# Routing weights through memory instead of through a product: one change to a GRU scan with a mixture of experts beside it

## The reference

```python
def cell(h, x):
    gi = x @ W_ih + b_ih
    gh = h @ W_hh + b_hh
    ...
    h_new = (1.0 - z) * n + z * h
    return (h_new, h_new)
...
scores = jax.nn.sigmoid(jnp.dot(xf, gate_w.T))
topv, topi = jax.lax.top_k(scores, 2)
topv = topv / topv.sum(axis=-1, keepdims=True)
dw = jnp.zeros((T, E)).at[jnp.arange(T)[:, None], topi].add(topv)
y0 = _mlp(xf, sw1, sw2, sw3)
def step(y, ws):
    e1, e2, e3, we = ws
    return (y + _mlp(xf, e1, e2, e3) * we[:, None], None)
```

## Time and profile before

| | us |
|---|---|
| median of 3 runs (lowest, highest) | 2738.11 (2737.35, 2738.44) |
| the profiled execution's own time | 2739.84 |
| its span in the profile | 2737.9 |
| first to last scan product (L1152) | 652.0 to 2584.5 |
| PE busy | 2545.8 (93%) |
| DVE, ACT, POOL busy | 1973.0, 1051.1, 1164.3 |
| moved by DMA | 209.39 MB |

### The profile page before, as it was taken

How to read it: one execution, slowest core, us unless ns; L and a number is a source line. 1 busy time by engine, 2 the same in 40 slices (tenths; PEclk the granted TensorE clock), 3 DMA queues, 4 the chain that set the end, 5 groups by cost and what they waited for, 6 DMA issues and landing times.

```text
span 2737.9 us, 159456 instructions
## 1 busy us (share of the span) xinstructions
PE 2545.8 (93%) x69506; PEld 1992.5 (73%) x69506; DVE 1973.0 (72%) x7088; ACT 1051.1 (38%) x3585; POOL 1164.3 (43%) x2972
## 2 busy tenths in 40 slices
PE   5777778787999999999999999999999999999999
PEld 2333333445888788888888888888888888888888
DVE  3767777774666777777787778878777777877722
ACT  4271625263333333333333333333333333333333
POOL 1232221222332455455545555554555555455454
PEclk9799989899999999999999999999999999999999
DMA  4100000001111233233333333333332333222344
GB/s 168 36 22 17 2 17 3 2 3 33 39 50 48 79 96 95 83 106 93 96 96 95 94 87 106 93 96 99 93 98 83 106 93 97 89 90 85 85 153 133
DMA packets 144746, 209.39 MB, mean 76 GB/s; under 512 B 16432, under 2 KB 86320, under 8 KB 143664
## 3 DMA queue, kind: packets, MB, share of 16 engines
q1 hardware_dynamic: 142896, 195.01, 23.3%
q10 hardware_dynamic: 1152, 4.19, 0.4%
HBM read 185.51 MB, written 13.63 MB: 73 GB/s over the span
## 4 chain that ended last, share of the span: by engine, by line
PE 70%; DVE 3%; issue 1%; POOL 1%; ACT 1%; DVEq 0%; POOLq 0%; ACTq 0%
PE ps L1152 27%; PE ps L1187 24%; PE ps L1202 12%; PE ps L1164 6%; PE ps L1176 2%; POOL hidf L844 0%; DVE turn_n L1033 0%; DVE turn L1036 0%; DVE fresh L1046 0%; DVE hcur L1048 0%; DVE hcur L1051 0%; DVE npre L1039 0%; ACT cand L940 0%; DVE h L1049 0%; DVE up L1020 0%
## 5 line engine op out<-in xcount | busy, mean ns | idle before, releaser
L1152 PE MATMUL ps<-whh,hcur 128*32 128x128 f16 x49152 | 791.5, 220 | 23.8 <-DVE hcur L1051 12.3
L1152 PEld LDWEIGHTS ps<-whh,hcur 128*32 128x32 f16 x49152 | 694.3, 97 | 147.0 <-DVE hcur L1051 119.4
L1187 PE MATMUL ps<-hb,w 128*128 128x256 f16 x6400 | 781.8, 273 | 0.0
L1187 PEld LDWEIGHTS ps<-hb,w 128*128 128x128 bf16 x6400 | 602.9, 98 | 95.1 <-DMA w<-in_w 0.3
L836 POOL COPY hb<-hcur 128x32 f16<-128x32 f16 x512 | 169.8, 332 | 664.2 <-DVE hcur L1051 664.2
L1202 PE MATMUL ps<-hid,w 128*128 128x256 f16 x3200 | 428.3, 273 | 2.2 <-POOL hid L856 1.8
L933 ACT ACTIVATE r<-ur 128x16 f32<-128x16 f32 x512 | 110.6, 216 | 825.5 <-DVE ur L1027 825.5
L1202 PEld LDWEIGHTS ps<-hid,w 128*128 128x128 bf16 x3200 | 312.3, 98 | 39.8 <-issue 3.0
L844 POOL TENSOR_TENSOR hidf<-up 128x256 f32<-128x256 f32 x400 | 291.8, 730 | 98.1 <-POOL hid L856 50.5
L856 POOL TENSOR_TENSOR hid<-hidf,hid 128x256 f16<-128x256 f32 x400 | 269.0, 673 | 62.3 <-ACT hid L929 62.3
L1024 DVE STREAM_TRANSPOSE turn<-ps 128x128 f32<-128x128 f32 x512 | 161.8, 316 | 179.4 <-PE ps L1152 168.9
(11 more groups left out here) (143 smaller groups left out, 3277.7 us busy)
## 6 DMA issues: line engine op xcount, KB each, us to landing
w<-in_w SPq DMA_DIRECT2D x400, 256.0 KB, 2.7
w<-in_w SPq DMA_DIRECT2D x400, 128.0 KB, 2.7
gi_scratch<-gis SPq DMA_DIRECT2D x72, 128.0 KB, 1.7
spare<-gi_scratch SPq DMA_DIRECT2D x36, 128.0 KB, 2.8
gi<-gi_scratch SPq DMA_DIRECT2D x36, 128.0 KB, 2.7
x2T<-in_xT SPq DMA_DIRECT2D x4, 1024.0 KB, 7.7
out<-xo ACTq DMA_DIRECT2D x8, 512.0 KB, 4.4
stage<-in_W_hh SPq DMA_DIRECT2D x1, 3072.0 KB, 11.1
```

What stands on the lines that cost most here:

```text
L1152: mm = pe.matmul(ps[j * COLS:(j + 1) * COLS, bank, 0:P], hcur[:, k], whh[:, s, k, at:at + P], start=(k + s == 0), stop=(k == KT - 1 and s ...
L1187: mm = pe.matmul(ps[:, UB[u], w * TOK:(w + 1) * TOK], w13[:, u, w, k], hb[:, f % 2, s, k].rearrange("p b t -> p (b t)"), start=(w + k + s ...
```

## The change

The weights stay float32: `dwT` is 16x256, copied once from PSUM (`weights_out`, ACT, step 7), and ACT itself sends it to a scratch tensor in memory, `dw_scratch`. SP then loads for each expert chunk the row of its expert into all 128 partitions of one of six slots of `wsb` (128 KB written); where a chunk holds the end of one expert and the start of the next (12 of 44), two loads do it. The load for chunk c + 1 stands in SP's queue behind `w2_load` of chunk c. `weigh`, `share`, `weights_low`, the table `owner`, its load at the start and the zeroing of `dwT` go, and `DOWNS` no longer counts the pairs.

```diff
-HIDS, W2S = 10, 12
+HIDS, W2S, WSS = 10, 12, 6
...
+        dw_dram = nc.dram_tensor("dw_scratch", (2, E, TOK), F32, kind="Internal").ap()
...
-        owner = sb("owner", [P, NCH - SCH, P], BF16)
-        dwT = sb("dwT", [P, TOK], F16)
-        wsb = sb("wsb", [P, 2, 2 * TOK], F32)
+        dwT = sb("dwT", [E, TOK], F32)
+        wsb = sb("wsb", [P, WSS, TOK], F32)
...
-            shares = sum(1 for at in WEIGH if EXPERTS <= at <= i)
-            total = UP * NCH - UPS[EXPERTS - 1] + DOWN * NCH - LATE + NWG - 1
-            downs = -(-total * (i - EXPERTS + 1) // (TB - EXPERTS)) - (UPS[i] - UPS[EXPERTS - 1]) - shares
+            total = UP * NCH - UPS[EXPERTS - 1] + DOWN * NCH - LATE
+            downs = -(-total * (i - EXPERTS + 1) // (TB - EXPERTS)) - (UPS[i] - UPS[EXPERTS - 1])
...
+        NX = NCH - SCH
+        SPLIT = [min(P, (x * P // TOPI + 1) * TOPI - x * P) for x in range(NX)]
...
-            for dst, src in ((gwf[:], a["gate"]), (ne[:], a["ne"]), (identf[:], a["identf"]), (owner[:], a["owner"])):
+            for dst, src in ((gwf[:], a["gate"]), (ne[:], a["ne"]), (identf[:], a["identf"])):
...
+            def wsb_load(f, x):
+                xn = f * NX + x
+                if xn >= WSS:
+                    before = xn - WSS
+                    sp.wait_ge(up2_done, before // NX * NCH + SCH + before % NX + 1)
+                sp.wait_ge(dwT_sent, (f + 1) * 16)
+                e, s = x * P // TOPI, SPLIT[x]
+                sp.dma_start(wsb[0:s, xn % WSS], dw_dram[f % 2, e:e + 1].to_broadcast([s, TOK])).then_inc(wsb_in[xn % WSS], 16)
+                if s < P:
+                    sp.dma_start(wsb[s:P, xn % WSS], dw_dram[f % 2, e + 1:e + 2].to_broadcast([P - s, TOK])).then_inc(wsb_in[xn % WSS], 16)
...
                     w2_load(n)
+                    if SCH <= c + 1 < NCH:
+                        wsb_load(f, c + 1 - SCH)
                     if c % 4 == 2 and f + 2 < NBLK:
...
-            nc.gpsimd.memset(dwT[:], 0.0).then_inc(dwT_zero, 1)
...
-            def share(f, p):
-                n = f * NWG + p
-                act.wait_ge(weighed, n + 1)
-                act.wait_ge(up2_done, f * NCH + SCH + 2 * (p - 1))
-                nc.scalar.copy(wsb[:, (p + SCH // 2) % 2], ps[:, WB, :]).then_inc(wsb_done, 1)
...
-            def weights_high(f):
+            def weights_out(f):
                 act.wait_ge(turned, f + 1)
-                nc.scalar.copy(dwT[0:E], ps[0:E, WB, 128:128 + TOK]).then_inc(dwT_hi, 1)
+                need(act, dwT_sent, f * 16)
+                nc.scalar.copy(dwT[:], ps[0:E, WB, 128:128 + TOK]).then_inc(dwT_out, 1)
+                act.wait_ge(dwT_out, f + 1)
+                act.dma_start(dw_dram[f % 2], dwT[:]).then_inc(dwT_sent, 16)
...
                 if c >= SCH:
-                    dve.wait_ge(wsb_done, f * NWG + (c - SCH) // 2 + 1)
-                    nc.vector.tensor_tensor(up2[:], ps[:, UB[c % 2], TOK:2 * TOK], wsb[:, (c // 2) % 2, (c % 2) * TOK:(c % 2 + 1) * TOK],
-                                            ALU.mult).then_inc(up2_done, 1)
+                    xn = f * NX + c - SCH
+                    dve.wait_ge(wsb_in[xn % WSS], loads_until(xn) * 16)
+                    nc.vector.tensor_tensor(up2[:], ps[:, UB[c % 2], TOK:2 * TOK], wsb[:, xn % WSS], ALU.mult).then_inc(up2_done, 1)
...
-            def weights_low(f):
-                dve.wait_ge(dwT_hi, f + 1)
-                nc.vector.tensor_tensor(dwT[LOW:LOW + E], ps[0:E, WB, 128:128 + TOK], dwT[0:E], ALU.subtract).then_inc(dwT_lo, 1)
...
-            def weigh(f, p):
-                if p == 0:
-                    pe.wait_ge(dwT_hi, f + 1)
-                    pe.wait_ge(dwT_lo, f + 1)
-                need(pe, wsb_done, f * NWG + p)
-                for c in range(2):
-                    mm = pe.matmul(ps[:, WB, c * TOK:(c + 1) * TOK], owner[:, 2 * p + c], dwT[:],
-                                   start=(c == 0), stop=True, skip_group_check=True)
-                mm.then_inc(weighed, 1)
```

More of the change, by code:

```diff
@@ L18 @@
 NCH = SCH + E * TOPI // P
-NWG = (NCH - SCH) // 2
 PAIRS = TB // 2
-LOW = 64
 HALF = 2.0 ** 15
@@ L50, in build @@
         gi_dram = nc.dram_tensor("gi_scratch", (NBLK, P, M3, B * TB), F32, kind="Internal").ap()
+        dw_dram = nc.dram_tensor("dw_scratch", (2, E, TOK), F32, kind="Internal").ap()
         nc.disable_value_cache = True
         attention(nc, a, ps, x2T, whh, wih, bias, spare, h)
-        scan_and_ffn(nc, a, ps, x2T, whh, wih, bias, spare, h, gi_dram)
+        scan_and_ffn(nc, a, ps, x2T, whh, wih, bias, spare, h, gi_dram, dw_dram)
 def attention(nc, a, ps, x2T, whh, wih, bias, spare, h):
@@ L651, in _, with scan_and_ffn @@
                 pass
-def scan_and_ffn(nc, a, ps, x2T, whh, wih, bias, spare, h, gi_dram):
+def scan_and_ffn(nc, a, ps, x2T, whh, wih, bias, spare, h, gi_dram, dw_dram):
     with ExitStack() as ctx:
@@ L703, in scan_and_ffn @@
         route = sb("route", [P, 2, E], F32)
-        init_in, gw_hi, gw_ready, dwT_zero, h_zero = sem("init_in"), sem("gw_hi"), sem("gw_ready"), sem("dwT_zero"), sem("h_zero")
+        init_in, gw_hi, gw_ready, h_zero = sem("init_in"), sem("gw_hi"), sem("gw_ready"), sem("h_zero")
         gi_in = [sem("gi_in0"), sem("gi_in1")]
@@ L715, in scan_and_ffn @@
         r_ready, z_ready, cand_ready, copied = sem("r_ready"), sem("z_ready"), sem("cand_ready"), sem("copied")
-        up_done, weighed, down_done = sem("up_done"), sem("weighed"), sem("down_done")
-        wsb_done = sem("wsb_done")
+        up_done, down_done = sem("up_done"), sem("down_done")
+        wsb_in = [sem("wsb_in%d" % n) for n in range(WSS)]
         sg_done, up1_done, up2_done, hidf_done, hid_hi, hid_lo = (
@@ L720, in scan_and_ffn @@
         logit_done, logit_ready, scored, rstep = sem("logit_done"), sem("logit_ready"), sem("scored"), sem("rstep")
-        routed, turned, dwT_hi, dwT_lo = sem("routed"), sem("turned"), sem("dwT_hi"), sem("dwT_lo")
+        routed, turned, dwT_out, dwT_sent = sem("routed"), sem("turned"), sem("dwT_out"), sem("dwT_sent")
         passed = sem("passed2")
@@ L749, in scan_and_ffn @@
         GATE = [2, 3, 4, 6, 7, 8] + [EXPERTS + n * (TB - EXPERTS) // (NCH - SCH) for n in range(NCH - SCH)]
-        WEIGH = [GATE[SCH + 2 * p] - 1 for p in range(NWG)]
         gate_at = [[c for c in range(NCH) if GATE[c] == i] for i in range(TB)]
-        weigh_at = [[p for p in range(NWG) if WEIGH[p] == i] for i in range(TB)]
         LEFT = [4, 3, 4, 4, 3, 5, 4, 3, 2]
@@ L772, in scan_and_ffn, with loads_until @@
         assert DOWNS[-1] == DOWN * NCH - LATE
+        NX = NCH - SCH
+        SPLIT = [min(P, (x * P // TOPI + 1) * TOPI - x * P) for x in range(NX)]
+        def loads_until(xn):
+            return sum(1 if SPLIT[v % NX] == P else 2 for v in range(xn % WSS, xn + 1, WSS))
         block = ctx.enter_context(nc.Block())
@@ L968, in _ @@
                         if i == TURN:
-                            weights_high(f)
+                            weights_out(f)
                         if i == RESULT + 1 and f >= 1:
@@ L976, in _ @@
                             sigmoid(f, c)
-                        for p in weigh_at[i]:
-                            share(f, p)
                     if g + 1 < S:
@@ L983, in _ @@
             for c in range(NCH):
-                if c >= SCH and c % 2 == 0:
-                    share(f, (c - SCH) // 2)
                 sigmoid(f, c)
@@ L1004, in split_router @@
             def split_router():
-                dve.wait_ge(init_in, 4 * 16)
+                dve.wait_ge(init_in, 3 * 16)
                 nc.vector.tensor_copy(gw[:, :, 0], gwf[:]).then_inc(gw_hi, 1)
@@ L1122, in _ @@
                             next(routing)
-                        if i == TURN + 1:
-                            weights_low(f)
                         if i == RESULT and f >= 1:
@@ L1223, in logits @@
                 if f == 0:
-                    pe.wait_ge(init_in, 4 * 16)
+                    pe.wait_ge(init_in, 3 * 16)
                     pe.wait_ge(gw_ready, 1)
-                    pe.wait_ge(dwT_zero, 1)
                     pe.wait_ge(g_out, GATES)
-                need(pe, wsb_done, f * NWG)
+                need(pe, dwT_out, f)
                 for t in range(2):
@@ L1257, in _ @@
                         turn_weights(f)
-                    for p in weigh_at[i]:
-                        weigh(f, p)
                     take(ups, UPS[i] - (UPS[i - 1] if i else 0))
@@ L1272, in _ @@
             for c in range(2, NCH):
-                if c >= SCH and c % 2 == 0:
-                    weigh(f, (c - SCH) // 2)
                 take(ups, UP)
@@ L1312 @@
     r = np.arange(P)
-    owner = np.zeros((P, E * TOPI), w13.dtype)
-    for e in range(E):
-        owner[e, e * TOPI:(e + 1) * TOPI] = 1
-    owner[LOW:LOW + E] = owner[0:E]
     sel = np.repeat((r[:, None] % 32 == 4 * np.arange(QT) + r[:, None] // 32)[:, :, None], P, axis=2).astype(np.float16)
@@ L1331 @@
         "gate": rows(np.asarray(L0_ffn_gate_w).T[unit]),
```

(2 more changed lines are left out.)

1 line of the change is left out of this document (removed).

## The result

The changed kernel takes 2782.07 us (median of 4 runs, 2776.72 to 2789.74) against 2737.73 for the kernel before beside it: 44 us more, ratio 1.0164, 95% interval 1.014 to 1.0188. The forecast was 2727, its range ended at 2752. The profiled execution is the longest of the four, 2789.74 with a span of 2787.7, so the trace shows some 8 us more loss than the median. Two later executions that took 6656 and 6249 us (one of four in experiment 4, one of ten in experiment 8), where the others of the same kernel took under 2800, are left out of the medians.

A forecast was written before the change was run, and what follows sets the result against it. TensorE was taken to bound the kernel, scan steps lying within 0.2 us of both PE's work and the recurrence. Terms -21.1 - 4.8 + 1.5 + 12 + 1 = -11.4 on 2739.8 gave 2728.4, at the median 2727; range 2711 to 2752.

The forecast's parts named there:

- Contention: +1 us: Mid-scan: PE's 22.7 us of unexplained waits may grow with a fifth more DMA traffic; +1 us.
- The broadcast loads, +12: Scan: rows land in 3.3 us, a third of 105 narrow chunks stall DVE by 0.35 us each; +12 us.
- The products in the scan, -21.1: Scan: without the owner pairs, 21 steps a block shorten and more nine-unit steps follow each other; -21.1 us.
- step 7, +1.5: ACT's wait and DMA issue in step 7 cost 2.8 us, removing weights_low in step 8 gives 1.3; +1.5 us.
- The two floors: Scan step: PE's work, 3.75 us with ten units, and the recurrence, about 3.57 us whatever PE does.
- the count of turned steps: Scan, steps 10 to 63: 21 steps a block turn from 3.75 into 3.63 us, leaving 22 of ten units.
- Pass 7, -4.8: Last pass, no recurrence: 22 owner pairs removed at 0.22 us each; -4.8 us.
- Pass 7, late rows: 0: Last pass: rows come a microsecond late each time, but downs and ups run later, so it costs 0.
- the 2.4 that the forecast gave as cover: Last pass: up products wait for L1020 of two chunks before, with 2.4 us; longer delays stall each chunk.
- PE waits for w13 or POOL's low half in pass 7: Last pass: a sign that, if it appeared, would make the prediction wrong.
- Slower: Rival: surcharge by rows or queued reads of one address; 2750 us at 3.7 us landing, 2778 at 4.3; chance 0.20.
- All hidden: Rival: broadcasts land like any load, in 2.7 to 3.0 us, giving 2715 us; chance 0.24.

The follow-up runs named there:

- experiment 4: Kernel before, plus the same number of broadcast loads at the same places, into a tile nobody reads: 2793.12 us, 54.2 above before.
- experiment 8: Changed kernel with w2 loaded only twelve times and then reused, all broadcast loads kept: 2734.06 us, 4.6 below before.
- experiment 1: Changed kernel with only the first six broadcast loads, later chunks reusing those rows: 2719.94 us, 19.0 below before.
- experiment 2: Changed kernel with each load reading 128 different rows of 1 KB instead of one row 128 times: 2741.62 us, 2.7 above before.
- experiment 6: Changed kernel, loads issued one chunk earlier and, in the scan, only after SP waits for the next step's z products: 2767.19 us, 29.1 above before.
- experiment 7: Changed kernel with each load reading 512 B from each of 128 different rows: 2728.27 us, 9.8 below before.
- experiment 5: Changed kernel with each broadcast load issued one chunk earlier: 2780.89 us, 42.8 above before.
- experiment 9: Kernel before with one owner product per expert, 8 pairs a pass instead of 22, no memory round trip: 2727.74 us, 10.4 below before.
- experiment 3: Changed kernel with broadcast rows of 512 B instead of 1 KB, still from one address: 2769.49 us, 30.6 above before.

## Why the prediction was wrong

**The step that failed is "Contention: +1 us".** It named the right row, PE's waits "that nothing in the profile explains, mid-scan", and priced the growth at 1 us for a fifth more traffic. Against experiment 1 the loads cost 63 us: 21.7 for bytes (experiment 2) and 41.6 for the one address. In the window the issue waits grew by 53 us, in the scan's products, where each one holds the recurrence. The trace puts a price on them: measured against the medians of experiment 1 at the same positions, the 142 steps of after with such a stall are 69.0 us longer and all other steps together 9.8; in experiment 1 itself it is 13.6 us in 41 steps, and 4.7. The error was to scale an unexplained wait by mean traffic. Half of the row's 22.7 us lies in block 0 besides, in waits of at most 0.5 us, where no expert's weights are loaded. The growth goes with what the DMA engines have to do at the moment when TensorE's next instructions are due, as the next paragraph shows.

What is shown of that, and what is inferred. Shown: loads that touch nothing of TensorE's make its scan stall (experiment 4), less queued at once makes fewer stalls (6, 7, 8), late rows make at most a small part of the loss (4, 5), and every stall stands where a new block of 256 instructions begins. From the trace, read packet by packet, between block 1 and the end of the scan: nearly nine stalls in ten (36 of 42 before, 126 of 142 after) end 1.25 to 1.6 us after a 16 KB packet of the instruction queue ends, and such a packet takes 1.08 us on the mean before and 1.07 after. So the packets aren't slower, they begin late. From the moment when TensorE enters one block to the begin of the packet for the next, the median is 1.17 us where no stall follows and 1.90 where one does. And it depends on the data: after, where the DMA engines were busy with data for under a tenth of the first microsecond of that time, a stall followed in 7 of 89 cases, and where it was four tenths or more, in 135 of 270. With different rows (experiment 2) it was 62 of 272 in the busier case, and 28 of 222 before, so how busy the engines are isn't all of it. Inferred: that the late packets stood behind data in their own DMA engine. The trace doesn't say what a packet waited for.

The Trainium skill (Runtime: NRT & Kernel Launch, Instruction fetch mechanics) has the sequencer refill its instruction memory by a DMA queue of its own in 16 KiB blocks of 256 instructions, the cost of a crossing "mostly hidden". The trace agrees on the block: q8 has 392 packets and 6.42 MB in the window, 16.4 KB each, and 6.42 MB over the 99,715 products and weight loads are 64 bytes each, so the queue is TensorE's. The stalls at every 256th instruction say the same. On the cost it agrees only while the data queues are short: 11.4 us at 94 GB/s, 64.3 with the change.

**The broadcast loads, +12, on DVE.** The landing was right: 3.3 forecast, 3.4 in the scan.

```profile
L805 SPq DMA_DIRECT2D wsb<-dw_scratch x298: 324/376/2198, 935.2 to 2576.6; - x149
...
DMA to landing us min/median/max: 1.8/3.4/4.9
```

The prediction's estimate by the row-pitch figures of the Trainium skill (DMA: Bandwidth & Descriptors, Latency and other measured facts) was 3.1; the trace is slower than that. Experiment 2 shows that the surcharge of 0.7 us over different rows is real. The waits that followed were right in sum too, 11.1 us, though in 21 longer waits and not 35 of 0.35. What they cost was less. Experiment 5 removes them and gains 1.5 us by the medians, some 10 at the most. In the trace, 17 of the 21 fall in steps without a stall of TensorE; they are 7.7 us of waits, and these 17 steps are 3.9 us longer than the medians of experiment 1. So the item of +12 was about right as a sum of waits and too large as a price, and it wasn't where the loss lay. What stands ahead of a load matters here too: without w2 (experiment 8) the row lands in 3.3 us instead of 3.5, and DVE's waits fall to 1.5 us.

**The products in the scan, -21.1, and step 7, +1.5.** By the steps' medians, seven times their sum fell from 1669.3 us to 1649.8 in experiment 1: -19.5 where -19.6 was forecast. The two floors hold, and so does the count of turned steps: by the medians of experiment 1, 22 of the 54 late positions take 3.7 us or more, 44 before. The item for step 7 came near by luck: of its +2.8 for ACT's write 1.3 came (step 8 went from 3.62 to 3.80 us, seven times 0.18), and its -1.3 for `weights_low` didn't come at all (the step behind it stayed at 3.58). Some of the gain was lost again to irregular steps, 18.3 us in experiment 1 against 12.4, which the forecast had put at nothing.

**Pass 7, -4.8.** From the last scan start to the end it is 150.0 us in experiment 1, 154.7 before: -4.7, right.

**Pass 7, late rows: 0.** Here it is 159.7 in the changed kernel and 155.1 in experiment 5, where nearly all rows come in time. DVE waited 83.7 us in 38 waits between 2590 and 2790, nearly all of it covered as argued, because the downs run behind. The cover ran out at some split chunks. Timeline of after:

```profile
2660.97 0.38 SPq L805 DMA_DIRECT2D wsb<-dw_scratch  x1
2661.39 0.43 SPq L807 DMA_DIRECT2D wsb<-dw_scratch  x1
...
2662.07 0.38 ACT L929 ACTIVATE sg<-ps 128x256 f32<-128x256 f32 x1 [1.53 <-PE ps L1175]
...
2665.93 0.42 DVE L1024 TENSOR_TENSOR up<-ps,wsb 128x256 f32<-128x256 f32 x1 [3.14 <-DMA wsb<-dw_scratch]
...
2666.83 0.60 PE L1175 MATMUL ps<-hb,w 128*128 128x256 f16 x4 [0.83 <-DVE up L1025]
```

The chunk whose sigmoid ended at 2662.45 is split. Its row was issued in two parts, at 2660.97 and 2661.39, and L1024 began only at 2665.93, 3.48 us after the sigmoid and beyond the 2.4 that the forecast gave as cover; PE waited 0.83 us for L1025 behind it. Such waits of PE for DVE sum to 1.8 us there, waits for w13 and for POOL's low half to 4.1 (1.8 before). The item is worth at most the 4.6 us between the two traces. The other 5 us up to experiment 1's 150.0 come without late rows, and the forecast had nothing for them. The named sign, "PE waits for w13 or POOL's low half in pass 7", did appear, at DMA 0.67 and 188 GB/s against a forecast that left the traffic out.

**The rivals.** "Slower" had a chance of 0.20 and was tied to landings of 3.7 us or more; landings were 3.4, for which the forecast has about no change. The time was nearest to it, 2782 against its 2750 and 2778, and the mechanism was another: that was luck. "All hidden" would have been right for DVE's waits alone. The range ended at 2752 because it had no case in which traffic itself holds TensorE, though the row for it had been read.

**What stays open.** Why 128 reads of one address take longer than reads of different rows was not settled: more bytes, more reads and one address were told apart, the place where they queue was not. That the stalls are waits for instructions is shown, that the packets were held up by data in their own DMA engine is inferred, as said. And no run has w2 away without the broadcasts, so the 14 to 33 us of experiment 8 stay an estimate.

## What to carry to other kernels

A load can cost more than its own landing time when TensorE runs a long unrolled program: look at its weight loads' waits for "issue" mid-stage, count whether they stand 256 instructions apart, and test by adding the planned transfers, into a tile that nobody reads, to the kernel as it is (experiment 4 would have given the answer alone). Replacing cheap products by a memory round trip trades 0.22 us of TensorE for traffic on the path of its own instructions; cutting the products themselves (experiment 9) kept over half of the gain without it. And a wait that the chain or the waits view credits is not yet a price: 11 us in the scan and 84 in the last pass, of which experiment 5 took away all but 9, were worth 1.5 us there, some 10 at the most.

## What the runs showed of the hardware

- 128 reads of 1 KB from one address landed in 3.5 us, from 128 rows in 2.8, in the same place of the same queue; the loads of w2 beside them took 3.1 against 2.8. At a mean DMA share of 0.40 in both, that difference cost 42 us in the kernel.
- Its price went by reads: 41.6 us with rows of 1 KB, 40.4 with rows of 512 bytes, for the same 448 transfers (experiments 2, 3 and 7).
- TensorE's instructions come in 16 KB packets of 256, one in 4.3 us here (392 in 1675), about one scan step's instructions. All stalls of over 0.12 us inside the scan's groups of weight loads stand at the first instruction of such a block: 42 before (12.2 us), 142 after (65.4 us, 0.46 on the mean), at full clock. The packet before them had begun late, 1.90 us after TensorE entered the block before, against 1.17 elsewhere.
- A broadcast of 128 KB for each chunk costs far more beside the 128 KB of w2 than without it: 63 us with w2, 14 to 33 without.
